# Attention slots of a four-layer fp32 kernel reordered: one late visit of PE to the small PSUM bank, the values product two slots behind the transposes

## The reference, cut to what matters

```python
xn = ln(x, g_norm)
q = (xn @ Wq).reshape(b, n, 16, 64).transpose(0, 2, 1, 3)
kv = xn @ Wkv; k, v = kv[..., :64], kv[..., 64:]   # plus one null key and value
q = l2norm(q) * q_scale; k = l2norm(k) * k_scale   # layer 0 only
sim = q @ k^T + bias            # causal, masked
out = softmax(sim) @ v          # (b, 16, n, 64)
x = x + ln(out.reshape(b, n, 1024) @ Wout, g_out)
```

## Time and profile before

| | us |
|---|---|
| median of 3 runs (1735.16 to 1735.62) | 1735.61 |
| profiled execution, time | 1732.54 |
| its span, first to last instruction | 1730.6 |
| busy PE / DVE / ACT / POOL | 1470.3 / 1410.4 / 1210.2 / 751.0 |
| stretch 89.6 to 741.1: attention layer 0 | 651.5 |
| stretch 741.1 to 1354.4: attention layer 1 | 613.3 |
| stretch 1354.4 to 1730.6: the two expert layers | 376.2 |

### The profile page before, as it was taken

How to read it: one execution, slowest core, us unless ns; L and a number is a source line. 1 busy time by engine, 2 the same in 40 slices (tenths; PEclk the granted TensorE clock), 3 DMA queues, 4 the chain that set the end, 5 groups by cost and what they waited for, 6 DMA issues and landing times.

```text
span 1730.6 us, 46424 instructions
## 1 busy us (share of the span) xinstructions
PE 1470.3 (85%) x16377; PEld 1081.0 (62%) x16377; DVE 1410.4 (81%) x3651; ACT 1210.2 (70%) x3064; POOL 751.0 (43%) x1412
## 2 busy tenths in 40 slices
PE   2467778888889999977888888999999799999998
PEld 1245556666677777766666666777777555555555
DVE  4557778888889999977788888999999687777777
ACT  1268778888889899978888888989999432332232
POOL 5557776443434334366554232223222365522222
PEclk9779999999999999989999999999999899999999
DMA  4002122111211223012121212221223000000000
GB/s 138 7 24 62 51 62 75 57 62 69 75 58 67 87 99 99 33 44 62 51 81 52 85 63 75 75 81 62 82 99 99 1 25 19 1 1 1 13 13 25
DMA packets 50440, 96.70 MB, mean 56 GB/s; under 512 B 3332, under 2 KB 27028, under 8 KB 50212
## 3 DMA queue, kind: packets, MB, share of 16 engines
q1 hardware_dynamic: 45504, 90.27, 15.8%
q10 hardware_dynamic: 4708, 3.45, 0.7%
HBM read 91.54 MB, written 2.17 MB: 54 GB/s over the span
## 4 chain that ended last, share of the span: by engine, by line
PE 42%; DVE 21%; ACT 14%; issue 11%; POOL 3%; DMA 1%; DVEq 0%; ACTq 0%; SPq 0%; POOLq 0%
PE tp L1312 7%; DVE p_lo L964 7%; ACT p_hi L722 6%; DVE biased L880 5%; PE sc L1203 3%; PE sc L1086 3%; PE sc L1087 3%; PE sc L1088 3%; ACT q_b L651 3%; PE sc L1204 3%; ACT probs L630 3%; PE op L1086 2%; PE aux L1086 2%; PE tp L1086 2%; PE aux L1088 2%
## 5 line engine op out<-in xcount | busy, mean ns | idle before, releaser
L964 DVE TENSOR_TENSOR p_lo<-tp,p_hi 128x512 f16<-128x512 f32 (+3 forms) x768 | 416.6, 554 | 121.3 <-ACT p_hi L722 114.3
L880 DVE CUSTOM_DVE_ANT_0 biased<-sc,bias,neg_null 128x256 f32<-128x256 f32 (+7 forms) x512 | 411.0, 803 | 2.7 <-issue 0.8
L630 ACT ACTIVATE probs<-biased,neg_max 128x256 f32<-128x256 f32 (+7 forms) x512 | 395.7, 773 | 14.2 <-DVE neg_max L880 12.7
L1312 PE MATMUL tp<-ident,probs 128*128 128x128 f32 x2304 | 388.7, 278 | 17.7 <-DVE p_lo L964 15.5
L722 ACT ACTIVATE p_hi<-tp 128x512 f16<-128x512 f32 (+3 forms) x768 | 368.9, 491 | 43.6 <-PE tp L1312 33.5
L1086 PE MATMUL op<-v_s,p_hi 128*128 128x64 f16 x2304 | 284.9, 194 | 54.4 <-DVE p_lo L964 35.9
L1203 PE MATMUL sc<-k_a,q_a 128*128 128x512 f16 (+3 forms) x768 | 254.2, 331 | 66.2 <-DVE neg_max L880 59.3
L1312 PEld LDWEIGHTS tp<-ident,probs 128*128 128x128 f32 x2304 | 267.9, 142 | 52.9 <-issue 37.9
L1088 PE MATMUL op<-v_s,p_lo 128*128 128x64 f16 x2304 | 284.0, 194 | 0.0
L1087 PE MATMUL op<-v_s,p_hi 128*128 128x64 f16 x2304 | 283.9, 194 | 0.0
L1086 PEld LDWEIGHTS op<-v_s,p_hi 128*128 128x128 f16 x2304 | 216.0, 99 | 85.5 <-DVE p_lo L964 62.1
(11 more groups left out here) (257 smaller groups left out, 3611.4 us busy)
## 6 DMA issues: line engine op xcount, KB each, us to landing
bias<-rel_table SPq DMA_DIRECT2D x4, 2048.0 KB, 8.5
bias<-in_fside_16xSxS SPq DMA_DIRECT2D x4, 2048.0 KB, 7.9
bias<-rel_table SPq DMA_DIRECT2D x4, 1792.0 KB, 7.9
bias<-in_fside_16xSxS SPq DMA_DIRECT2D x4, 1792.0 KB, 7.1
bias<-rel_table SPq DMA_DIRECT2D x4, 1536.0 KB, 7.3
bias<-in_fside_16xSxS SPq DMA_DIRECT2D x4, 1536.0 KB, 6.7
bias<-rel_table SPq DMA_DIRECT2D x4, 1280.0 KB, 5.6
bias<-in_fside_16xSxS SPq DMA_DIRECT2D x4, 1280.0 KB, 6.3
```

The source lines that it names most:

```text
L630: ac.activation(probs[:, i % 2, 0:w], biased[:, i % 2, 0:w], ACT.Exp, bias=neg_max[:, u % 2, i % HU:i % HU + 1], scale=-1.0, accum_out=row ...
L880: ve.tensor_tensor_reduce(out=biased[:, i % 2, 0:w], in0=sc[i % 2][:, 0:w], in1=bias[:, g % 2, i % HU, 0:w], scale=-1.0, scalar=neg_null[: ...
L964: ve.tensor_tensor(p_lo[:, gi % 4, 0:nb * P], tp[gi % 2][:, 0:nb * P], p_hi[:, gi % 4, 0:nb * P], ALU.subtract).then_inc(s["p_lo"], 1)
L1312: last = te.transpose(tp[gi % 2][:, jj * P:(jj + 1) * P], probs[:, n % 2, (j0 + jj) * P:(j0 + jj + 1) * P], ident[:, :])
```

## The change

The same instructions, in another order within and across slots. The end of the pipeline comes one slot later (`LAST`).

- PE does its small piece once per slot, at the slot's **end**: k = 0 null products and y together (in one bank), k = 1 query projection, k = 2 transposes of q_n, k = 3 transposes of o_n. Only the three rare pieces of x, kv and k stay behind the first group.
- ACT evicts that piece **first** in the next slot, ahead of `probs`. DVE's ot_lo and neg_null move ahead of `p_lo`.
- The values product in slot n belongs to slot **n-2**. So o_raw, o_n, the query norm and the y statistics move one slot later.

The core of the diff (left out: the moved y statistics, the removed ACT and DVE blocks, which come back unchanged, and the body of the rare pieces):

```diff
@@ -235,7 +235,7 @@
 
         def free_banks(n):
 
-            return 0 <= n < N - 4 and all(plan.tile(i) < TILES // 2 for i in range(n + 1, n + 4))
+            return 0 <= n < N - 6 and all(plan.tile(i) < TILES // 2 for i in range(n + 1, n + 6))
 
...
@@ -367,7 +367,7 @@
         NU = N // HU
         U0 = NU // 2
         STEP_N = UNITS * HU
-        FIRST, LAST = -20, N + 8
+        FIRST, LAST = -20, N + 9
 
...
@@ -469,7 +469,7 @@
                 m, k = divmod(n, HU)
                 if TABLE_AT.get(n) == 4:
                     rel_rstd(1)
-                if k == 1 and 1 <= m <= NU:
+                if k == 2 and 1 <= m <= NU:
 
...
@@ -479,7 +479,7 @@
                     gp.tensor_tensor(o_n[:, :, :], o_raw[:, :, :],
                                      r_den[:, :].unsqueeze(2).to_broadcast([P, HU, DH]), ALU.mult)\
                         .then_inc(s["o_n"], 1)
-                if k == 2 and 0 <= m + 3 < U0:
+                if k == 3 and 0 <= m + 3 < U0:
 
...
@@ -617,6 +617,46 @@
                 if n in TABLE_AT:
                     table_stage(TABLE_AT[n])
                 first, second = banks(n)
+                was_first, was_second = banks(n - 1)
+                if k == 1 and 0 <= m - 2 < NU:
+                    u = m - 2
+                    act.wait_ge(s["y"], u + 1)
+                    if u % UNITS < B:
+                        if u >= UNITS:
+                            act.wait_ge(s["x_new"], (u // UNITS - 1) * B + u % B + 1)
+                        dst = y_acc[:, u % B, :]
+                    else:
+                        if y_adds(u) >= 2:
+                            act.wait_ge(s["y_acc"], y_adds(u) - 1)
+                        dst = y_s[:, :]
+                    ac.activation(dst, was_first[:, 0:D], ACT.Copy, scale=1.0 / WS).then_inc(s["y_s"], 1)
+                if k == 3 and 0 <= m + 2 < NU:
+                    u = m + 2
+                    act.wait_ge(s["q_t"], u + 1)
+                    if u >= 2:
+                        act.wait_ge(s["scores"], HU * (u - 1))
+                    for e in range(2):
+                        ac.activation(heads(q_b[0:DH, u % 2, :], e),
+                                      was_first[e * DH:(e + 1) * DH, 0:UW].rearrange("p (c q) -> p c q", q=P), ACT.Copy)\
+                            .then_inc(s["q_hi"], 1)
+                    act.wait_ge(s["q_hi"], 2 * (u + 1))
+                    ac.activation(q_a[0:DH, u % 2, :], q_b[0:DH, u % 2, :], ACT.Copy).then_inc(s["q_dup"], 1)
+                if k == 2 and 0 <= m + 3 < NU:
+                    u = m + 3
+                    act.wait_ge(s["q_proj"], u + 1)
+                    if u < U0:
+                        if u >= 1:
+                            act.wait_ge(s["q_ss"], u)
+                        ac.activation(q_sq[:, :, :].rearrange("p h d -> p (h d)"), was_first[:, 0:UW], ACT.Square)\
+                            .then_inc(s["q_sq"], 1)
+                    ac.activation(q_n[:, u % 2, :], was_first[:, 0:UW], ACT.Copy, scale=1.0 if u < U0 else DH ** -0.5 / WS)\
+                        .then_inc(s["q_na"], 1)
+                if k == 0 and 0 <= m - 2 < NU:
+                    u = m - 2
+                    act.wait_ge(s["ot"], u + 1)
+                    o_t = was_first[:, 0:UW].rearrange("p (c q) -> p c q", q=P)
+                    ac.activation(ot_hi[:, :].rearrange("p (c q) -> p c q", q=P), turned(o_t) if u < U0 else o_t,
+                                  ACT.Copy).then_inc(s["ot_hi"], 1)
                 i = n + 1
                 if 0 <= i < N:
...
@@ -852,10 +853,11 @@
                 if n in TABLE_AT:
                     table_stage(TABLE_AT[n])
                 first, second = banks(n)
-                if k == 1 and 1 <= m <= NU:
+                was_first, was_second = banks(n - 1)
+                if k == 2 and 1 <= m <= NU:
                     u = m - 1
                     dve.wait_ge(s["o_null"], u + 1)
-                    dve.wait_ge(s["pv"], plan.groups_done(n - 2))
+                    dve.wait_ge(s["pv"], plan.groups_done(n - 3))
                     ve.tensor_tensor(o_raw[:, :, :], op[:, 0:UW].rearrange("p (h d) -> p h d", h=HU),
                                      o_null[:, :, :], ALU.add).then_inc(s["o_raw"], 1)
...
@@ -906,14 +908,33 @@
                     dve.wait_ge(s["q_hi"], 2 * (u + 1))
                     for e in range(2):
                         ve.tensor_tensor(heads(q_a[DH:P, u % 2, :], e),
-                                         first[e * DH:(e + 1) * DH, 0:UW].rearrange("p (c q) -> p c q", q=P),
+                                         was_first[e * DH:(e + 1) * DH, 0:UW].rearrange("p (c q) -> p c q", q=P),
                                          heads(q_b[0:DH, u % 2, :], e), ALU.subtract).then_inc(s["q_lo"], 1)
+                if k == 1 and 0 <= m + 1 < NU:
+
+                    u = m + 1
+                    hg = (u % UNITS) // B
+                    dve.wait_ge(s["q_null"], u + 1)
+                    if 0 <= m - 2 < NU:
+                        dve.wait_ge(s["y_s"], m - 1)
+                    if u >= 2:
+                        dve.wait_ge(s["d_null"], u - 1)
+                    ve.scalar_tensor_tensor(neg_null[:, u % 2, :], was_first[:, UW:UW + HU], -1.0,
+                                            null_b[u // U0][:, hg * HU:(hg + 1) * HU], ALU.mult, ALU.subtract)\
+                        .then_inc(s["null"], 1)
+                if k == 0 and 0 <= m - 2 < NU:
+                    u = m - 2
+                    dve.wait_ge(s["ot_hi"], u + 1)
+                    o_t = was_first[:, 0:UW].rearrange("p (c q) -> p c q", q=P)
+                    ve.tensor_tensor(ot_lo[:, :].rearrange("p (c q) -> p c q", q=P), turned(o_t) if u < U0 else o_t,
+                                     ot_hi[:, :].rearrange("p (c q) -> p c q", q=P), ALU.subtract)\
+                        .then_inc(s["ot_lo"], 1)
                 def small():
 
                     for T in range(STEPS):
                         n0 = T * STEP_N
                         layer, t = divmod(T, TILES)
-                        if n == n0 - 15:
+                        if n == n0 - 14:
                             dve.wait_ge(s["xt_hi"], T + 1)
                             if layer == 0:
...
+                            for bt in range(B):
+                                last = te.transpose(second[:, bt * P:(bt + 1) * P], k_d[:, bt, :], ident[:, :])
+                            last.then_inc(s["kt"], 1)
+
+                now, before = plan.at(n), plan.at(n - 2)
+                for j in range(max(1, len(now), len(before))):
+                    if j < len(now):
+                        gi = now[j]
+                        _, j0, nb = plan.groups[gi]
+                        pe.wait_ge(s["probs"], n + 1)
+                        if gi >= 2:
+                            pe.wait_ge(s["p_lo"], gi - 1)
+                        for jj in range(nb):
+                            last = te.transpose(tp[gi % 2][:, jj * P:(jj + 1) * P],
+                                                probs[:, n % 2, (j0 + jj) * P:(j0 + jj + 1) * P], ident[:, :])
+                        last.then_inc(s["pt"], 1)
+                    if j < len(before):
+                        pv(before[j])
+                    if j == 0:
+                        small()
+                if k == 0:
+                    after = []
+                    if 0 <= m - 2 < NU:
+                        after.append((s["y_s"], m - 1))
+                    if 0 <= m + 1 < NU:
+                        after.append((s["null"], m + 2))
+                    take(False, *after)
+                if k == 0 and 0 <= m + 1 < NU:
+                    u = m + 1
+                    layer = u // U0
+                    pe.wait_ge(s["q_dup"], u + 1)
+                    pe.wait_ge(s["q_lo"], 2 * (u + 1))
+                    if u == 0:
+                        pe.wait_ge(setup["big"], 1)
+                    for h in range(HU):
+                        cols = slice(h * P, (h + 1) * P)
+                        te.matmul(first[:, UW + h:UW + h + 1], q_a[:, u % 2, cols], kn_a[:, layer:layer + 1], start=True, stop=False)
+                        last = te.matmul(first[:, UW + h:UW + h + 1], q_b[:, u % 2, cols], kn_b[:, layer:layer + 1],
+                                         start=False, stop=True)
+                    last.then_inc(s["q_null"], 1)
                 if k == 0 and 0 <= m - 2 < NU:
                     u = m - 2
                     layer, hg = u // U0, (u % UNITS) // B
-                    take(False, (s["y_s"], u + 1))
                     pe.wait_ge(s["ot_lo"], u + 1)
                     if u % U0 == 0:
...
                     last.then_inc(s["y"], 1)
-                if k == 3 and 0 <= m + 2 < NU:
+                if k == 2 and 0 <= m + 2 < NU:
                     u = m + 2
                     take(False, (s["q_lo"], 2 * (u + 1)))
                     pe.wait_ge(s["q_na"], u + 1)
@@ -1245,77 +1317,14 @@
```

(20 more changed lines are left out.)

155 lines of the change are left out of this document (35 added, 120 removed).

## The result

The changed kernel takes 1891.9 us, the median of four runs (1889.4 to 1893.9), against 1735.6 before on the same chip: ratio 1.0896, 95% interval [1.0877, 1.0916]. It is slower, as forecast, but by 156 us and not by 54, and so outside the range of 1742 to 1822. The profiled execution has a span of 1886.6 us, 156.0 more than before.

A forecast was written before the change was run, and what follows sets the result against it. The longest ring of waits closing once per attention unit bounds the kernel. Layer 1's 32 us and layer 0's 23 gave 1732.5 + 55 = 1787.5, and 3.1 more for the median gave 1790 us; own range 1765 to 1815, overall 1742 to 1822.

The forecast's parts named there:

- Step sizes and the check on tile 3: Step times read from rows; walked through the kernel before's tile 3 they gave 8.50 us per unit against 8.49 measured.
- Tiles 0, 3, 5 and 7: Layer 1's distance between two q_a in these tiles grows to about 6.1, 8.9, 11.3 and 13.2 us.
- the layer-1 sum for steady units: Layer 1: 8 units times the added us per unit of its eight tiles, 32 us slower.
- Tile 4's "about no change": Tile 4's side branch gives 10.5 us per unit: about no change, bounds -0.2 and +0.4.
- The guard: Tile 7: guarding the bank by columns would close the unit at 13.0 us; by the bank rule 13.2 stands.
- "Rare pieces ... taken as 0, since they delay the kernel before as well": Norm statistics, x and kv: 0 to 1 us in each of 16 steps, taken as 0.
- "Layer 0 ... I take 23": Layer 0, with POOL's query norm one slot later in front of d_null: 23 us slower, bounds 10 and 40.
- "about 6.9 in tile 0": Layer 0's tile 0: the ring through POOL's query norm and d_null takes about 6.9 us per unit.
- Rival 3: POOL's later query norm blocks ACT in every layer-0 unit, rare pieces add their full 16 us: 1823; chance 0.12.
- Walking rings of units only: The method: the longest ring of waits closing once per unit of four slots decides the time.
- the faster rival: PE's 59.3 + 35.9 us of waits go and nothing replaces them: 1688, or about 1710; chance 0.16.

The follow-up runs named there:

- e2: Changed kernel with ACT doing probs ahead of its four evictions; ratio 1.0897 to the kernel before.
- e9: Changed kernel with only DVE's ot_lo moved in slot 0, ahead of `biased` and xn; ratio 1.0681 to the kernel before.
- e5: Changed kernel with o_n's transposes of the narrow tiles in half bank `second` instead of `aux`; ratio 1.1026 to the kernel before.
- e1: Changed kernel with POOL's query norm of slot 3 moved behind d_null, denom and o_null; ratio 1.0823 to the kernel before.
- e14: Changed kernel with product one slot behind, POOL's query norm behind d_null, DVE's evictions first, rare pieces ahead of the slot's first group; ratio 1.0296.
- e12: Changed kernel with values product one slot behind, POOL's query norm behind d_null and DVE's three evictions first; ratio 1.0318 to the kernel before.
- e10: Changed kernel with o_n's transposes of the narrow tiles in the upper half of sc[0]; ratio 1.0925 to the kernel before.
- e18: e14 with three overwritten transposes more per slot in tiles 0 to 3, where PE waits for probs; ratio 1.0315 to the kernel before.
- e13: Changed kernel with rare pieces ahead of the slot's first group on PE, ACT and DVE; ratio 1.0911 to the kernel before.
- e11: Changed kernel with product one slot behind, POOL's query norm behind d_null, ot_lo alone first, ACT's q_b and q_a behind probs; ratio 1.046.
- e8: Kernel before with only o_n's transposes, ot_hi and ot_lo moved from slot 2 to slot 3; ratio 1.0829 to the kernel before.
- e16: Kernel before with POOL's query norm in slot 3, ahead of d_null; ratio 1.0006 to the kernel before.

## Why the prediction was half right

1. *Step sizes and the check on tile 3*: held. They carried over to the changed kernel within 0.15 us in four tiles.
2. *Tiles 0, 3, 5 and 7* (6.1, 8.9, 11.3, 13.2): right (6.17, 8.92, 11.35, 13.34), and so is the layer-1 sum for steady units (32; 35.4). Tile 4's "about no change" holds (-0.02 in its steady unit). In tile 7 this isn't luck: the rows have the walked ring. DVE's p_lo starts at 1448.20, `biased` at 1449.41, ot_lo at 1450.61; PE's null products, after 0.20 us of waiting for it, at 1451.08, y at 1451.30; and ACT goes from the p_hi that waits for a product through q_b, q_a and probs to the next p_hi without a gap, the 3.08 us shown under e2. e9 takes ot_lo out of this ring and the unit loses 0.37. In tile 3 e2 took off 0.2 us, which the walk doesn't explain.
3. *The guard*: the null products wait for ot_lo 12.7 us in all, 0.7 at most, and the unit came to 13.34, on the side of 13.2 and not of 13.0. The order to wait is the program's own, so this doesn't test the rule of the Trainium skill (PSUM — Partial Sum Buffer, PSUM bank collisions raise a hardware error) that two engines may not be in one bank on the same partitions at once, whatever the columns. What obeying it costs when the null products are behind ot_lo is what e5 measured in the narrow tiles: 23 us.
4. *"Rare pieces ... taken as 0, since they delay the kernel before as well"*: the first step that failed, and the larger, with its bounds of 0 to 1 us per step. In layer 1 they are 24 us, 3 per step, and in layer 0 some 36, 4.5 per step: 60 us where the sum has none. The reason given, that they delay the kernel before as well, is true of what they took before and says nothing of what is added. The sentence named xn between `biased` and ot_lo. That is a part: the units with xn hold 5.5 of layer 1's 24 us beyond the steady growth, e9 takes 12.4 us off them in both layers, and e1, where rstd comes later still, adds 10.7 in layer 0. The wait for rstd itself, 1.3 us in the rows above, is hardly longer than before in total (7.9 us; 6.1). The other units, with y's statistics, keys and values, and the keys' transposes, were not walked at all. In wide tiles PE there waits 23.2 us in `aux` behind the rare pieces. Moving the rare pieces ahead gained 10 us in wide tiles and lost 7 in narrow ones (e14 against e12). So the failed step is known, and of its mechanism only a part; what makes up the rest of the 60 is open.
5. *"Layer 0 ... I take 23"*, bounds 10 and 40: the second: 88.6 measured, of which 36 are the rare pieces, so that 52 stand against the 23. It had to hold at least what layer 1's steady units have, 32, and I set it lower because I counted POOL's delay against the steady ring and called it hidden. Layer 0 has 29 us more than layer 1, 27 of them in tiles 0 to 3. POOL's order explains some 12 (e1 in layer 0). The walk's one figure for this layer, "about 6.9 in tile 0", was 8.74, and 7.35 in e1. Rival 3 (1823) had the right causes, was near with 17 us for POOL, and had too small a price for the rare pieces, 16 us at most; it too is 69 us short. The four misses are 3 us (layer 1's steady units), 29 (layer 0's), 60 (rare pieces) and 8 (ahead of the first q_a and behind the last): 100 of the 101 us between 55 and 156.
6. *Walking rings of units only.* The ring through o_n's transposes and q_lo, which makes the largest wait, was not in the walk. It cost nothing by itself in the narrow tiles (e10), so leaving it out wasn't the error there, but I would have read it as the cause from the list of waits alone. In tile 7's steady unit PE stands 0.86 us in it, beside the ring that binds.
7. *Against the faster rival*: right. PE's waits for `biased` and `p_lo` went, as it says, and others took their place.

What stays open is the rest of e14, 51 us over the kernel before. By q_a distances 35 lie in layer 0 (26 of them in its tiles 0 to 3), 8 in layer 1, and the others at both ends. It isn't the clock alone (e18), the rare pieces' place (e13) or POOL's order. What e14 still shares with the changed kernel is the visit at the slot's end, ACT's evictions in front and o_n's transposes in slot 3. Only ACT's order was taken away by itself (e2, and q_b and q_a in e11), without a clear gain; the other two were not. The last, costly in e8, is the likelier, but this is argued, not shown. No version beat the kernel before; e16 equals it.
